# Mixture-of-experts kernel on one core: expert scores summed from head output and x parts, roots on ScalarE, a reordered stretch before the experts

## What is computed

```
x = x + L0_xattn(_layernorm(x), ctx, ctx, igate_w, igate_b, fgate_w, fgate_b, ln_scale)
#   h  = (C / normalizer) @ v             per head, with decay weights D = exp(log_D - max)
#   out = (h - mean(h)) / sqrt(var(h) + 1e-5) * ln_scale
x = x + L0_ffn(_layernorm(x), expert_tokens, W1, b1, W2, b2, W3, b3)
#   scores = einsum('bnd,ed->bne', x, expert_tokens);  _, topk_idx = top_k(scores, 2)
#   outputs += mean(topk_idx == i) * mlp_i(x)              for each of the 8 experts
```

## Time and profile before

| What | us |
|---|---|
| median of 3 runs | 172.62 |
| lowest and highest | 172.21 and 174.15 |
| the profiled execution | 174.71 |
| its span | 173.0 |
| TensorE busy in the span | 156.5 |
| VectorE, ScalarE, GpSimd busy | 123.7, 112.3, 98.9 |

### The profile page before, as it was taken

How to read it: one execution, slowest core, us unless ns; L and a number is a source line. 1 busy time by engine, 2 the same in 40 slices (tenths; PEclk the granted TensorE clock), 3 DMA queues, 4 the chain that set the end, 5 groups by cost and what they waited for, 6 DMA issues and landing times.

```text
span 173.0 us, 3136 instructions
## 1 busy us (share of the span) xinstructions
PE 156.5 (90%) x1005; PEld 130.6 (75%) x1005; DVE 123.7 (72%) x370; ACT 112.3 (65%) x233; POOL 98.9 (57%) x132
## 2 busy tenths in 40 slices
PE   7897799999999699999999999999999999999700
PEld 2492337776668357899899999999999999999600
DVE  0849486888888875999987959959779599543300
ACT  2275586646575544896967969879789698754300
POOL 8899000131246899700878777687687741838270
PEclk9999999999999969999999999999999999999995
DMA  5489406999999310000112223122031120313031
GB/s 144 129 243 378 120 12 209 378 368 366 369 367 325 101 49 0 0 0 4 30 38 29 36 37 28 38 21 46 13 32 40 23 23 0 30 13 30 8 38 11
DMA packets 19339, 17.84 MB, mean 103 GB/s; under 512 B 2136, under 2 KB 13912, under 8 KB 19320
## 3 DMA queue, kind: packets, MB, share of 16 engines
q1 hardware_dynamic: 15408, 15.21, 26.8%
q0 software_dynamic: 3520, 2.30, 11.0%
q10 hardware_dynamic: 392, 0.10, 0.3%
HBM read 14.75 MB, written 2.75 MB: 101 GB/s over the span
## 4 chain that ended last, share of the span: by engine, by line
PE 63%; DVE 16%; ACT 5%; issue 4%; POOL 4%; DMA 3%; POOLq 1%; SPq 1%; ACTq 0%; DVEq 0%
PE bank L1364 41%; PE bank L1228 6%; PE bank L1197 4%; PE bank L1289 3%; DMA cs_in<-in_ctx 3%; DVE wlo L850 2%; PE bank L1421 2%; PE bank L1216 2%; POOL out_rows L513 2%; PE bank L1217 1%; PE bank L1353 1%; DVE g1l L1062 1%; ACT RH L581 1%; POOLq L63 1%; DVE oha L934 1%
## 5 line engine op out<-in xcount | busy, mean ns | idle before, releaser
L513 POOL DMA_INDIRECT out_rows<-ys,ids x24 | 39.1, 1628 | 21.8 <-DVE ys L1073 12.8
L1364 PE MATMUL bank<-g1h,whi 128*128 128x320 f32 x128 | 40.4, 316 | 0.4 <-DVE g1l L1062 0.3
L1364 PE MATMUL bank<-g1l,whi 128*128 128x320 f32 x128 | 39.5, 309 | 0.0
L1364 PE MATMUL bank<-g1h,wlo 128*128 128x320 f32 x128 | 39.5, 309 | 0.0
L701 ACT ACTIVATE g<-bank,smt 128x320 f32<-128x320 f32 x63 | 32.0, 530 | 8.5 <-PE bank L1364 7.4
L850 DVE TENSOR_TENSOR wlo<-wraw,whi 128x512 fp32r<-128x512 f32 x48 | 30.7, 685 | 1.6 <-ACT whi L618 1.3
L500 POOL DMA_INDIRECT xg<-xn_rows,ids x18 | 19.9, 1106 | 14.9 <-DVE ids L1032 9.7
L618 ACT ACTIVATE whi<-wraw 128x512 fp32r<-128x512 f32 x48 | 27.7, 632 | 0.8 <-PE bank L1289 0.8
L1364 PEld LDWEIGHTS bank<-g1h,whi 128*128 128x128 f32 x128 | 24.0, 188 | 1.1 <-issue 1.0
L1364 PEld LDWEIGHTS bank<-g1h,wlo 128*128 128x128 f32 x128 | 24.1, 188 | 0.0
L1364 PEld LDWEIGHTS bank<-g1l,whi 128*128 128x128 f32 x128 | 24.0, 188 | 0.0
(11 more groups left out here) (196 smaller groups left out, 312.1 us busy)
## 6 DMA issues: line engine op xcount, KB each, us to landing
wraw<-in_L_ffn_W SPq DMA_DIRECT2D x8, 1024.0 KB, 9.3
wraw<-in_L_ffn_W SPq DMA_DIRECT2D x16, 256.0 KB, 8.5
xs<-in_x SPq DMA_DIRECT2D x2, 256.0 KB, 3.3
cs_in<-in_ctx SPq DMA_DIRECT2D x2, 256.0 KB, 5.1
out_rows<-cs_in SPq DMA_DIRECT2D x8, 64.0 KB, 2.6
xn_rows<-qn SPq DMA_DIRECT2D x8, 64.0 KB, 2.4
out_rows<-ys,ids POOLq DMA_INDIRECT x24
xg<-xn_rows,ids POOLq DMA_INDIRECT x18
```

Of the source, the lines that this page charges most:

```text
L513: g.indirect_dma_start(out=out, out_offset=bass.IndirectOffsetOnAxis(ap=ids[0:n, col:col + 1], axis=0), in_=ys[0:n, e % 2, c, :], in_offse ...
L1364: last = t.matmul(dst, wcol(w, p, layer, k, m), act_(k), start=(n == 0), stop=(n == 3 * (1 if layer == 1 else MC) - 1))
```

## The change

The expert tokens are centred in both forms (with and without the learned scale) before the masked queries, and transposed on TensorE behind the gate logits (`ett`). `scores_x` forms the x part of all scores with eight products in the middle of the fillers of the start. In the loop TensorE transposes the head output (`h_transpose`) one pair earlier than it transposed x2; VectorE adds rs2 times its score to the x part (`sx`). All later roots are a logarithm and an exponential on ScalarE (`rsqrt`). GpSimd writes the normalised rows of pairs 0 to 2 and makes the choices for expert 0, batches 0 to 5; ScalarE makes those for expert 1, batches 0 to 3; VectorE writes the last pair's rows and makes the other choices, four of them behind `low_x(0)`. TensorE's list before the experts is rewritten, with three gathers of expert 1 before `layer1(0)` instead of four. The one-hot columns `oha` now lie in the decay buffer.

```diff
-WARM = {"inputs": 8, "context": 6, "gate weights": 2, "gate scans": 8, "gate rows": 14}
+WARM = {"inputs": 8, "context": 6, "gate weights": 2, "gate scans": 3, "gate maxima": 5, "gate rows": 12}
...
-            def rsqrt(dst, src, wait, done, j):
-                pool.wait_ge(wait, j + 1)
-                g.tensor_tensor(dst[:, 2 * j:2 * j + 2], src[:, 2 * j:2 * j + 2], minus_half[:, 0:2], ALU.pow)\
-                    .then_inc(done, 1)
-
-            def negative_mean(j):
+            def norm2(j):
 
                 pool.wait_ge(s.rs3_done, j + 1)
                 for b in (2 * j, 2 * j + 1):
-                    g.tensor_scalar(nb3[:, b:b + 1], mv3[:, b, 0:1], rs3[:, b:b + 1], -1.0, ALU.mult, ALU.mult)\
-                        .then_inc(s.nb3_done, 1)
+                    g.tensor_scalar(xn[:, b, :], x2[:, b, :], mv3[:, b, 0:1], rs3[:, b:b + 1], ALU.subtract, ALU.mult)\
+                        .then_inc(s.xn_done, 1)
...
-                g.tensor_scalar(chosen(1, b), places[:], selv[:, 1, b:b + 1], None, ALU.is_equal).then_inc(s.sel1_pool, 1)
+                g.tensor_scalar(chosen(0, b), places[:], selv[:, 0, b:b + 1], None, ALU.is_equal).then_inc(s.sel0_pool, 1)
...
-                rsqrt(rs2, ve2, s.ve2_done, s.rs2_done, j)
-                if j == NP - 2:
-                    choose_rows(0)
-                    choose_rows(1)
-                if j == NP - 1:
-                    place_tokens(1)
-                rsqrt(rs3, ve3, s.ve3_done, s.rs3_done, j)
-                negative_mean(j)
-                if j == NP - 2:
-                    place_tokens(0)
+            norm2(0)
+            norm2(1)
+            choose_rows(0)
+            choose_rows(1)
+            choose_rows(2)
+            choose_rows(3)
+            norm2(2)
+            choose_rows(4)
+            choose_rows(5)
+            place_tokens(0)
+            place_tokens(1)
...
+            act.wait_ge(s.ett_ps, 2)
+            a.activation(ett[:].rearrange("p n e -> p (n e)"), misc[:, 200:216], ACT.Copy).then_inc(s.ett_done, 1)
...
-            def keep_x2T(j):
...
-            def norm2(j):
-                act.wait_ge(s.nb3_done, 2 * j + 2)
-                for b in (2 * j, 2 * j + 1):
-                    a.activation(xn[:, b, :], x2[:, b, :], ACT.Identity, bias=nb3[:, b:b + 1], scale=rs3[:, b:b + 1])\
-                        .then_inc(s.xn_done, 1)
+            def keep_hT(j):
+                act.wait_ge(s.hT_ps, j + 1)
+                a.activation(hT[:], score_bank(j)[:, 0:2 * S].rearrange("p (i t) -> p i t", t=S), ACT.Copy)\
+                    .then_inc(s.hT_done, 1)
+
+            def rsqrt(n, j, ready):
+
+                act.wait_ge(ready, 2 * j + 2)
...
+                a.activation(ln[:, pair], mv[:, pair, 1], ACT.Ln, bias=epscol[:]).then_inc(s.ln_done, 1)
+                act.wait_ge(s.ln_done, LN_ORDER.index((n, j)) + 1)
+                a.activation(rs[:, pair], ln[:, pair], ACT.Exp, scale=-0.5).then_inc(done, 1)
...
-                if j >= 2:
-                    keep_x2T(j - 2)
-                if j == NP - 1:
-                    choose_rows(0)
                 if j == 0:
                     weights_hi(0, 2, [1, 2, 3])
+                    act.wait_ge(s.const_zero, 12)
                 elif j == 1:
                     select_heads(4)
                 elif j == 2:
                     select_heads(6)
+                if j >= 2:
+                    rsqrt(1, j - 2, s.mv3_done)
+                if j == NP - 1:
+                    act.wait_ge(s.rank_ps, 2)
+                    a.activation(rank_sb[:].rearrange("p b e -> p (b e)"), rank_cols(0, 2), ACT.Copy).then_inc(s.rank_kept, 1)
                 decay(2 * j + 1)
+                if j >= 1:
+                    rsqrt(0, j - 1, s.mv2_done)
+                    keep_hT(j - 1)
                 if j == 0:
                     weights_hi(0, 3)
                     select_heads(3)
...
                 elif j == 2:
                     select_heads(7)
-                if j >= 2:
-                    norm2(j - 2)
+            choose_rows(0)
             choose_rows(1)
-            act.wait_ge(s.rank_ps, 2)
-            a.activation(rank_sb[:].rearrange("p b e -> p (b e)"), rank_cols(0, 2), ACT.Copy).then_inc(s.rank_kept, 1)
-            keep_x2T(NP - 2)
-            norm2(NP - 2)
+            rsqrt(1, NP - 2, s.mv3_done)
             choose_rows(2)
-            keep_x2T(NP - 1)
+            keep_hT(NP - 1)
+            rsqrt(0, NP - 1, s.mv2_done)
             choose_rows(3)
-            norm2(NP - 1)
+            rsqrt(1, NP - 1, s.mv3_done)
...
+            dve.wait_ge(s.small_in, 16 * 4)
+            dve.wait_ge(s.bias_in, 48)
+            for n in range(2):
...
+                v.tensor_reduce(etsum[:, n:n + 1], ets[:, n, :], axis=AX.X, op=ALU.add).then_inc(s.et_done, 1)
+                dve.wait_ge(s.et_done, 3 * n + 1)
+                v.scalar_tensor_tensor(out=ets[:, n, :], in0=etsum[:, n:n + 1].to_broadcast([NE, D]), scalar=-1.0 / D,
+                                       in1=ets[:, n, :], op0=ALU.mult, op1=ALU.add).then_inc(s.et_done, 1)
...
+            v.tensor_tensor(std1[:], ve1[:], rs1[:], ALU.mult).then_inc(s.sx_done, 1)
+            dve.wait_ge(s.sx_done, 1)
+            dve.wait_ge(s.sx_ps, 1)
+            v.tensor_tensor(sx[:], bank[6][:, 0:B * NE].rearrange("p (b e) -> p b e", e=NE),
+                            std1[:].unsqueeze(2).to_broadcast([128, B, NE]), ALU.mult).then_inc(s.sx_done, 1)
...
+            def residual_and_choose(j):
                 p = j % 2
...
+                pair = slice(2 * j, 2 * j + 2)
+                dve.wait_ge(s.rs2_done, j + 1)
+                dve.wait_ge(s.hl_done, 2 * j + 2)
+                for b in (2 * j, 2 * j + 1):
+                    v.scalar_tensor_tensor(out=x2[:, b, :], in0=hl[:, p, b % 2, :], scalar=rs2[:, b:b + 1],
+                                           in1=xs[:, b, :], op0=ALU.mult, op1=ALU.add).then_inc(s.x2_done, 1)
+                dve.wait_ge(s.score_ps, j + 1)
+                for b in (2 * j, 2 * j + 1):
+                    v.scalar_tensor_tensor(out=sx[:, b, :], in0=score_bank(j)[:, 256 + 8 * (b % 2):264 + 8 * (b % 2)],
+                                           scalar=rs2[:, b:b + 1], in1=sx[:, b, :], op0=ALU.mult, op1=ALU.add)\
+                        .then_inc(s.sum_done, 1)
+                for b in (2 * j, 2 * j + 1):
+                    dve.wait_ge(s.sum_done, b + 1)
+                    v.max(top[:, b, :], sx[:, b, :]).then_inc(s.top_done, 1)
...
+                dve.wait_ge(s.mask_done, 2 * j + 1)
+                v.tensor_tensor(maskb[:, pair, :], ohk[:, pair, 0, :], ohk[:, pair, 1, :], ALU.add)\
+                    .then_inc(s.mask_done, 1)
+            def norm2(j):
+                dve.wait_ge(s.rs3_done, j + 1)
+                for b in (2 * j, 2 * j + 1):
+                    v.tensor_scalar(xn[:, b, :], x2[:, b, :], mv3[:, b, 0:1], rs3[:, b:b + 1], ALU.subtract, ALU.mult)\
+                        .then_inc(s.xn_last, 1)
...
-                if j >= 3:
-                    rows_wanted(j - 3)
                 weigh(2 * j)
+                if j >= 2:
+                    rows_wanted(j - 2)
...
-                    residual_and_choose(j - 1, j - 2)
+                    residual_and_choose(j - 1)
             normalise(NP - 1)
-            rows_wanted(NP - 3)
-            residual_and_choose(NP - 1, -1)
-            residual_and_choose(-1, NP - 2)
-            residual_and_choose(-1, NP - 1)
             rows_wanted(NP - 2)
-            choose_rows(0, B - 4)
-            choose_rows(0, B - 3)
+            residual_and_choose(NP - 1)
+            norm2(NP - 1)
             rows_wanted(NP - 1)
             choose_rows(0, B - 2)
             choose_rows(0, B - 1)
-            for b in range(2, 6):
-                choose_rows(1, b)
...
-            choose_rows(1, B - 2)
-            choose_rows(1, B - 1)
+            for b in range(4, B):
+                choose_rows(1, b)
...
+            pe.wait_ge(s.et_done, 5)
+            pe.wait_ge(s.cT_done, 2)
+            for n in range(2):
+                t.transpose(misc[:, 200 + NE * n:200 + NE * n + NE], ets[:, n, :], identf[0:NE, 0:NE]).then_inc(s.ett_ps, 1)
+            def scores_x():
+                pe.wait_ge(s.ett_done, 1)
+                for b in range(B):
+                    last = t.matmul(bank[6][:, NE * b:NE * b + NE], qT[:, b, :], ett[:, 0, :], start=True, stop=True)
+                last.then_inc(s.sx_ps, 1)
...
+            def h_transpose(j):
+                pe.wait_ge(s.hn_done, j + 1)
                 if j == 0:
                     pe.wait_ge(s.smt_done, 1)
+                elif j == 1:
+                    pe.wait_ge(s.sum_done, 2)
+                    pe.wait_ge(s.selv_done, 1)
+                else:
+                    pe.wait_ge(s.cw_done, 2 * B - 2 if j == NP - 2 else 2 * B)
                 for i in range(2):
```

(55 more changed lines are left out.)

160 lines of the change are left out of this document (62 added, 98 removed).

## The result

| | before | changed |
|---|---|---|
| median | 173.81 (20 runs) | 175.14 (20 runs) |
| lowest and highest | 172.21 and 175.84 | 173.19 and 175.55 |
| profiled execution, its span | 174.71, 173.0 | 175.43, 173.2 |
| `xlo` of expert 0 ends | 67.02 | 66.61 (forecast 63.6) |
| full stretch of products starts | 84.37 | 85.22 (forecast 81.6) |

The account below looks back on a forecast made before the run. Before expert 0 starts at 67.02, TensorE was held by a serial chain and a low clock. Clock 2.0 and chain 1.4 give -3.4; +0.7 given back makes -2.7, so 172.62 becomes 169.9, range 168.9 to 172.3.

Parts of the forecast that it names:

- I take the clock as kept: Last gathers before expert 0: TensorE stays at full clock, four gathers at 0.53 instead of 4.13 together; gain 2.0.
- Rival A: The clock falls anyway, from narrow products and waits between the gathers; price 2.1, time 172.0, chance 0.15.
- what is given back: Behind `xlo` of expert 0, VectorE has four choices instead of two before it places tokens; costs 0.7.
- GpSimd's lists stay hidden: GpSimd's one-hot rows end at 75.3, when TensorE asks for them; 1 us late would cost 0.6 more.
- Rival C: GpSimd becomes the bound through slow normalisations (2.2 each), and the clock falls again; +2.9 net, 175.5, chance 0.06.
- the estimate of 0.3 each: The six normalisations, if on VectorE instead of GpSimd, at some 0.3 each; the sum up to 1.8 worse.
- The chain: Last `values` to `xlo` of expert 0: transposing the head output earlier shortens the chain; gain 1.4.
- rival B: VectorE's chain binds the loop, the mask 0.5 late in each of three rounds; +1.5, 171.4, chance 0.12.
- D: The clock falls at the narrow products of the start, slowing 17 fillers; +3.9 less 0.1, 173.7, chance 0.05.
- The wait before gather (0,5): Before the experts, TensorE waits for GpSimd's choice, a new wait of 0.4; the gather ends at 60.25.
- a root: Two ScalarE operations on 128x2 replace GpSimd's 0.77; 0.20 each, 0.45 with the hand-over, at most 0.9.
- the start: Expert-token work and eight narrow products replace some first fillers; costed at 0, bounds -0.2 to +0.3.

Follow-up runs that it names:

- 5: Changed kernel with gather (0,0) before the last `values`, gather (0,1) inside it, and five 512-column fillers in and around the narrow stretch; 176.29, ratio 1.0133.
- 7: As 5, without VectorE's choices of rows of expert 1 for batches 4 and 5; 174.94, ratio 1.0098.
- 8: As 5, with the eight first 512-column fillers as 32 of 128 columns; 176.75.
- 12: As 11, plus the five fillers and the second gather inside `values` from 5; 173.15, ratio 0.9922.
- 15: As 12, with GpSimd's `place_tokens(0)` back behind the choices, as in the changed kernel; 175.79, ratio 1.0091.
- 13: Kernel before with the seven fillers of 6, plus two more in the middle of each of its last two `values`; 173.56, ratio 0.9994.
- 14: As 13, with VectorE's two choices of rows of expert 1 ahead of `xlo`; 173.26, ratio 0.9977.
- 1: Changed kernel with gather (0,0) moved back in front of the last `values`; 174.44, ratio 1.004.
- 2: Changed kernel with three 512-column fillers added in front of the last `values`; 174.4, ratio 1.000.
- 4: As 1, with the last pair's root put before the copy of its transposed head output on ScalarE; 174.12, ratio 1.0009.
- 11: As 4, with VectorE's choices ahead of `xlo`, GpSimd's placing ahead, and the first fillers in more, narrower instructions; 174.19, ratio 0.9999.
- 6: Kernel before with seven 512-column fillers in its waits: five before the last transposes, one before gather (0,3), one before the ranks of pair 3; 173.9, ratio 1.0012.
- 9: Changed kernel with VectorE's four choices of rows of expert 1 moved ahead of `xlo`; 174.02, ratio 0.9977.

## Why the prediction was wrong

**Two steps failed.** The first is "I take the clock as kept", 2.0 of the 2.7. It counted the eleven gathers from 54.6 on and left out what stood before them: with gather (0,0) moved behind it, the last `values` closed a run of narrow products from 50.53. Wide products spread over that run make the clock stay up more often: with them 33 of 48 runs of the changed kernel's variants 5, 7, 8, 12 and 15 were high, and 21 of 25 of the kernel before's (13, 14); without, 5 of 20 and 24 of 121. A gather or three fillers alone did not do it (1, 2, 4 and 11: 6 of 48), nor did fillers in the waits (6: 4 of 12). For the kernel before the pair 6 and 13 isolates the wide products inside `values`; for the changed one 11 and 12 differ also by three fillers around the ranks, behind `values`. What else decides whether a given execution loses the clock, and at which place, stays open: in the profiles falls begin between 40.6 and 62, and two of them (one in 8, one in 14) come in spite of the wide products. One profile had one short fall at 62, which was read as the price of idle time that the change would take away; over the runs the kernel before is low in 58 of 121 executions and the changed one in 12 of 20. So the term of the sum was 2.0 and came out at about nothing.

Rival A, that the clock falls anyway, is what happened, and its 2.1 is what lies between the high and the low runs of the kernel before (172.9 and 175.0; 1.3 in the changed one). It named narrow products and waits together; the narrow products were those between the gathers, not those before them, and the clock stayed through waits of 0.50 and 1.05 in the twelfth. The rule cited there from the Trainium skill (TensorE: Matmul & The Clock Gate, "A second HAM failure mode: psum-queue depth-cycling") tells of idling between groups of products. The fall in the changed kernel came at 54.0, with TensorE busy 2.00 of 2.00 in the windows before and behind it; so the measurement goes beyond that rule.

**The second is "what is given back"**, mis-sized: 0.7 expected, 1.25 in the profile (18.55 against 17.30); moving the four choices away (9 against the changed kernel) was worth 1.35 of that way in the profiles and 1.5 in the ratios. The four choices behind `xlo` take 1.5, and VectorE has no slack there; but in front of `xlo` it waits 1.61, which the prediction did not see as a place for them. These rows of the changed kernel show both, and a place where TensorE waits for VectorE, at the `xlo` of expert 1:

```profile
66.12 0.49 DVE L1047 TENSOR_TENSOR xlo<-bank,xhi 128x320 fp32r<-128x320 f32 x1 [1.61 <-ACT xhi L716]
66.53 0.81 DVE L917 TENSOR_SCALAR qm<-places,selv 128x320 f32<-128x320 f32 x2
...
67.25 0.81 DVE L917 TENSOR_SCALAR dec<-places,selv 128x320 f32<-128x320 f32 x2
...
79.94 0.42 PE L1384 MATMUL bank<-xhi,whi 128*128 128x320 f32 x1 [0.54 <-DVE xlo L1047]
```

Behind this stood a wall that would have taken a part of the clock's gain too: "GpSimd's lists stay hidden", 75.3 against 75.3, and 0.6 for being 1 us late. Their end was right (75.5 in the changed kernel). But with `xlo` at 65, VectorE starts the 128x512 differences of the next weights at 73 to 75, and a one-hot row of 0.60 takes mostly 1.35 to 1.9 beside them. TensorE then waited 0.88 (5), 1.80 (7) and 1.74 (15) for the lists, and going from 12 to 15 cost 1.7%. SBUF — State Buffer (Who interferes with whom) of the Trainium skill says that a VectorE instruction with two inputs in SBUF contends with a GpSimd instruction that reads SBUF, over a port that one of them holds for a whole instruction. The trace agrees: the difference has two such inputs, and only beside it do GpSimd's rows take up to three times as long; beside the shorter differences of 128x320 they took up to 1.25 and 1.19 (changed). Rival C, GpSimd as the bound, was given 0.06 and priced through slow normalisations; they took 0.794, as forecast, and two of the same form on VectorE took 0.60 together (63.12 in the changed kernel), as the estimate of 0.3 each had it. Where the clock was kept and the lists came late, GpSimd did bind, by another door.

**What held.** The chain: in the eleventh, with the clock kept and 0.6 of gather in front, head transposes were at 56.5, scores ended at 58.7 and `xlo` at 64.4; the forecast with that 0.6 is 56.5, 58.5 and 64.2. So the shorter chain is worth nearly what was said, 1.2 of 1.4; the eleventh has the root, the choices and the placing moved too, so this is not the change's chain alone. The masks came in time: from 24 to 53 TensorE waited for no engine in the changed kernel (rival B did not happen), and the clock stayed at 1.00 from 14.6 to 50 (nor did D). The wait before gather (0,5) on GpSimd's choice appears only with the clock kept, 0.25 in 5. Two small misses: a root takes 0.29 + 0.20, not 2 x 0.20; and the start, costed at 0 with +0.3 as its end, moved the first exponents by 0.6 to 1.1, of which 0.2 reached the loop (values at 26.48 against 26.25).

**The ledger, an estimate.** Chain -1.2, clock 0, given back +1.25 to +1.5, start +0.2: +0.3 to +0.5, against +1.1 measured (0.6 to 1.6). The rest, 0.6 to 0.8, I have not placed; a part may be GpSimd's lists in those runs in which `xlo` came early. What lies around the span is 2.2 in the changed kernel and 1.7 to 1.9 before, but from the last transposes to the end of the execution both profiled runs take about the same, 10.9 (175.43 less 164.52, changed) and 11.1 (174.71 less 163.62, before), so I do not count it.

The best version keeps the change and adds what the runs found (12). That it beats the kernel before is shown, by 0.8% [0.35%, 1.2%]; that the fillers earn more than they cost there (12 against 11) is likely and not shown by itself, since the intervals overlap.

## What to carry to other kernels

Ask of each stretch on TensorE not only whether it is busy but with what: in this kernel the clock fell behind a busy run of `values` with 17 columns each, and wide products put inside them (13) raised the share of high runs from 4 of 12 to 10 of 12. Read the clock from many executions, not from one profile. When a step is made earlier, list what starts earlier on the other engines with it, and what shares a port or a queue at that new time; and when an engine's work lands behind a critical step, look first whether it idles in front of it.
